# The first scores of each window with whole queries as weights and masked keys moving

## The reference

```
q, k, v = x @ wq.T + bq, x @ wk.T + bk, x @ wv.T + bv
scores  = 0 everywhere
scores[window n, window n] = q_w . k_w * 0.25      # windows of 128 tokens, 16 per batch
scores[g, g'] += q_g . k_g' * 0.25                 # 64 global tokens: every 32nd
out = softmax(scores) @ v @ wo.T + bo
x1  = layernorm(x + out)
```

## Time and profile before

| | us |
|---|---|
| median of three runs | 445.81 |
| lowest, highest | 444.01, 446.04 |
| span of the profiled execution | 442.8 |
| TensorE busy | 405.3 (92%) |
| VectorE busy | 326.1 (74%) |
| ScalarE busy | 250.6 (57%) |
| GpSimd busy | 220.4 (50%) |

### The profile page before, as it was taken

How to read it: one execution, slowest core, us unless ns; L and a number is a source line. 1 busy time by engine, 2 the same in 40 slices (tenths; PEclk the granted TensorE clock), 3 DMA queues, 4 the chain that set the end, 5 groups by cost and what they waited for, 6 DMA issues and landing times.

```text
span 442.8 us, 14658 instructions
## 1 busy us (share of the span) xinstructions
PE 405.3 (92%) x5747; PEld 339.8 (77%) x5747; DVE 326.1 (74%) x796; ACT 250.6 (57%) x523; POOL 220.4 (50%) x301
## 2 busy tenths in 40 slices
PE   5899799999999999999999899988798998999991
PEld 4758678888888888888888778756577887777891
DVE  6785687758757757757759888563668998899785
ACT  3424665675575575575576576676663555544421
POOL 4361343464464464464464566435733485477540
PEclk9999999999999999999999999999989999999997
DMA  8663740000000000000020000000000011011004
GB/s 240 186 199 111 240 137 4 27 25 0 24 24 0 24 24 0 24 24 0 24 72 4 25 2 3 3 1 2 0 2 2 1 49 47 0 47 49 34 15 143
DMA packets 21720, 20.34 MB, mean 46 GB/s; under 512 B 3133, under 2 KB 21682, under 8 KB 21682
## 3 DMA queue, kind: packets, MB, share of 16 engines
q1 hardware_dynamic: 16900, 15.07, 10.9%
q10 hardware_dynamic: 4782, 4.75, 3.3%
HBM read 15.41 MB, written 4.41 MB: 45 GB/s over the span
## 4 chain that ended last, share of the span: by engine, by line
PE 52%; DVE 26%; ACT 9%; issue 8%; DMA 3%; ACTq 1%; DVEq 0%; POOL 0%; POOLq 0%
DVE row_max_t L1154 10%; PE ps L1461 7%; PE ps L1737 7%; PE ps L1424 7%; PE ps L1562 5%; PE ps L1384 5%; PE ps L1415 4%; PE ps L1438 3%; PE ps L1444 3%; ACT probs L847 3%; DVE k_part L1013 2%; ACT boundsT_t L858 2%; PE ps L1406 2%; DMA rows<-in_L_attn_x_dram 2%; ACT k_part L713 2%
## 5 line engine op out<-in xcount | busy, mean ns | idle before, releaser
L847 ACT ACTIVATE probs<-ps 128x1024 f32<-128x1024 f32 x64 | 62.1, 1022 | 68.2 <-PE ps L1428 68.2
L1154 DVE TENSOR_REDUCE row_max_t<-ps 128x16 f32<-128x2048 f32 x31 | 70.9, 2287 | 3.7 <-PE ps L1415 3.6
L1737 PE MATMUL ps<-w_part,hm_part 128*128 128x256 f32 x384 | 53.8, 289 | 1.8 <-DVE hm_part L1332 1.8
L1415 PE MATMUL ps<-k_part,q_part 32*128 32x128 f32 x1584 | 51.5, 274 | 3.1 <-issue 1.5
L1415 PEld LDWEIGHTS ps<-k_part,q_part 32*128 32x128 f32 x1584 | 46.9, 186 | 9.2 <-issue 7.0
L1562 PE MATMUL ps<-xh_parts,w_part 128*128 128x512 f32 x192 | 53.8, 416 | 0.0
L557 POOL TENSOR_TENSOR q_part<-qf,q_part 128x512 fp32r<-128x512 f32 x32 | 41.0, 1281 | 25.7 <-ACT q_part L695 25.7
L599 POOL TENSOR_TENSOR attn_t<-num_t,rden_t 128x256 f32<-128x256 f32 x32 | 20.0, 624 | 64.7 <-DVE rden_t L1185 64.7
L1737 PEld LDWEIGHTS ps<-w_part,hm_part 128*128 128x128 f32 x384 | 48.2, 190 | 4.8 <-DVE hm_part L1332 2.4
L788 ACT ACTIVATE ffn_rows<-ps,b1s 128x512 f32<-128x512 f32 x32 | 22.0, 687 | 42.2 <-PE ps L1562 34.1
L1562 PEld LDWEIGHTS ps<-xh_parts,w_part 128*128 128x128 f32 x192 | 34.7, 194 | 6.5 <-issue 0.6
(11 more groups left out here) (234 smaller groups left out, 906.4 us busy)
## 6 DMA issues: line engine op xcount, KB each, us to landing
table<-rest_sums SPq DMA_DIRECT2D x4, 1088.0 KB, 6.1
xs<-in_L_attn_x_dram SPq DMA_DIRECT2D x16, 256.0 KB, 2.8
rows<-in_L_attn_x_dram ACTq DMA_DIRECT2D x4, 1024.0 KB, 8.1
out_dram<-yout SPq DMA_DIRECT2D x6, 512.0 KB, 2.9
w<-in_L_ffn_W_dram SPq DMA_DIRECT2D x2, 256.0 KB, 7.6
w<-in_L_ffn_W_dram SPq DMA_DIRECT2D x1, 512.0 KB, 4.2
out_dram<-yout SPq DMA_DIRECT2D x2, 256.0 KB, 2.6
out_dram<-yout ACTq DMA_DIRECT2D x2, 256.0 KB, 2.8
```

Of the source, the lines that this page charges most:

```text
L847: act.activation(probs[:, 2 * h:2 * h + 2, :], ps[:, 2 * h:2 * h + 2, :], ACT.Exp).then_inc(probs_ready, 1)
L1154: dve.tensor_reduce(row_max[:], ps_all, op=ALU.max, axis=AX.X).then_inc(max_ready, 1)
L1415: last = mm(ps[:, u, (2 * c + a) * P:(2 * c + a + 1) * P], q_part[x][quad(u), s, c, a, :], k_part[y][quad(u), s, c, :], start=(i == 0), st ...
L1737: mm(y, hm_part[a][:, 1 - p, f, c * P:(c + 1) * P], w2_part[b][:, f, :], start=(f == 0 and i == 0), stop=False)
```

## The change

The first scores take whole queries as weights and masked keys as the moving operand. The even and the odd head's keys lie side by side, 256 columns, so that one product gives two heads: 24 products in place of 48. The turned scores stay as they were, and so need masked queries too.

- ScalarE takes the query high part from PSUM with its bias (q_whole[0], two operations), now in even steps, after the exponential's argument and before the exponentials; its copy of qf in odd steps goes. VectorE takes the query remainder (q_whole[1], two operations) in place of the four of L1004, and waits for ScalarE's.
- VectorE masks the keys of the next pair (mask_keys: four tensor_scalar operations, high and low part, even and odd head) in odd steps after the guard.
- GpSimd masks the queries of the current pair (mask_queries: two tensor_scalar operations for the high part before the bounds, two for the low part after them) in even steps; q_low goes.
- The masked keys lie in the experts' xh_parts buffer, so the casts of the first group (take_high) move from step 30 to step 31; w_raw and dg change places.
- W1 lies in ysum and is loaded by SP at step 24, ahead of w2; its splitting moves to steps 26 to 28.

```diff
+        k_masked = [xh_parts[:, 0, i].rearrange("p c n -> p (c n)").rearrange("p (w c a n) -> p w c a n", w=2, c=KC, a=2)
+                    for i in range(2)]
-        qf = sb("qf", [P, 2, KC, 2, P])
+        q_whole = [sb(f"q_whole{i}", [P, SLOTS, KC, P], fp32r) for i in range(2)]
+                    for c in range(KC):                                   # SP, step 24
+                        sp.dma_start(w1[:, c, :, :], w1_dram[:, c * P:(c + 1) * P, :].rearrange("e p h -> p e h")).then_inc(ld_w1, 16)
-            def q_low(w, s):
-                need(pool, turned_scores_in_psum, w - 3)
-                pool.wait_ge(q_high_ready, w // 2 + 1)
-                pool.tensor_tensor(q_part[1][:, s], qf[:, s % 2], q_part[0][:, s].bitcast(fp32), ALU.subtract).then_inc(q_ready, 1)
+            def await_queries(w):
+                need(pool, turned_scores_in_psum, w - 2)
+                pool.wait_ge(q_ready, w // 2 + 1)
+            def mask_queries(i, s):
+                for a in range(2):
+                    pool.tensor_scalar(q_part[i][:, s:s + 2, :, a, :], q_whole[i][:, s:s + 2].bitcast(fp32), q_scale[:, a, 0:1], None,
+                                       ALU.mult).then_inc(q_masked_ready, 1)
...
             def queries_of(w, s):                                         # ScalarE
-                need(act, turned_scores_in_psum, w - 2)
-                act.wait_ge(qf_ready, w // 2 + 1)
-                copy(q_part[0][:, s:s + 2], qf[:]).then_inc(q_high_ready, 1)
+                need(act, turned_scores_in_psum, w - 3)
+                act.wait_ge(q_in_psum, w // 2 + 1)
+                for c in range(KC):
+                    last = act.activation(q_whole[0][:, s:s + 2, c, :], ps_xq[:, c * 2 * P:(c + 1) * 2 * P].rearrange("p (w n) -> p w n", w=2),
+                                          ACT.Identity, bias=bq_col[:, c:c + 1])
+                last.then_inc(q_high_ready, 1)
...
+            def queries_of(w, s):                                         # VectorE
+                dve.wait_ge(q_high_ready, w // 2 + 1)
+                for c in range(KC):
+                    last = dve.scalar_tensor_tensor(q_whole[1][:, s:s + 2, c, :], ps_xq[:, c * 2 * P:(c + 1) * 2 * P].rearrange("p (w n) -> p w n", w=2),
+                                                    bq_col[:, c:c + 1], q_whole[0][:, s:s + 2, c, :].bitcast(fp32), ALU.add, ALU.subtract)
+                last.then_inc(q_ready, 1)
+            def mask_keys(w, s):
+                need(dve, scores_in_psum, w)
+                dve.wait_ge(k_ready, w // 2 + 1)
+                for i in range(2):
+                    for a in range(2):
+                        dve.tensor_scalar(k_masked[i][:, :, :, a, :], k_part[i][:, s:s + 2].bitcast(fp32), q_scale[:, a, 0:1], None,
+                                          ALU.mult).then_inc(k_masked_ready, 1)
...
                 if ahead and p == 0:                                      # VectorE's step
-                    queries_of(t + AHEAD)
+                    queries_of(t + AHEAD, (s + AHEAD) % SLOTS)
+                if live(t + 1, steady) and p:
+                    mask_keys(t + 1, (s + 1) % SLOTS)
...
             def scores(s):                                                # TensorE
                 for c in range(KC):
+                    for i, (x, y) in enumerate(SPLIT):
+                        for u in range(UNITS):
+                            last = mm(ps[:, u, 2 * c * P:(2 * c + 2) * P], q_whole[x][quad(u), s, c, :],
+                                      k_masked[y][quad(u), s % 2, c, :, :].rearrange("p a n -> p (a n)"),
+                                      start=(i == 0), stop=(i == 2), tile_position=(32 * u, 0))
```

More of the change, by code:

```diff
@@ L503, in _ @@
             load_w(WO, wo_dram)
-            for c in range(KC):
-                sp.dma_start(w1[:, c, :, :], w1_dram[:, c * P:(c + 1) * P, :].rearrange("e p h -> p e h")).then_inc(ld_w1, 16)
             sp.dma_start(out_bias[:], bo_dram.rearrange("(a n) -> a n", a=1).broadcast_to([P, HID])).then_inc(ld_bo, 16)
@@ L574, in step @@
                 ahead, cur, pp, old, older = (live(t + k, steady) for k in (AHEAD, 0, -2, -3, -4))
+                queries_due = cur and p == 0 and (steady or t > 0)
+                if queries_due:
+                    await_queries(t)
                 if pp:
@@ L842, in step @@
                     keep_onehot(0, 0)
+                if ahead and p == 0:
+                    queries_of(t + AHEAD, (s + AHEAD) % SLOTS)
                 if prev:
@@ L1411, in scores, with scores_of_globals @@
                 for c in range(KC):
+                    for i, (x, y) in enumerate(SPLIT):
[3 more added lines that the diff above has]
+                                      start=(i == 0), stop=(i == 2), tile_position=(32 * u, 0))
+                return last
+            def scores_of_globals():
+                s = GSLOT
+                for c in range(KC):
                     for a in range(2):
@@ L1703, in _ @@
             pe.wait_ge(kg_ready, 1)
-            scores(GSLOT).then_inc(gs_in_psum, 1)
+            scores_of_globals().then_inc(gs_in_psum, 1)
             turn_x(2)
```

60 lines of the change are left out of this document (29 added, 31 removed).

## The result

464.24 us (median of 4 runs, 464.06 to 466.36) against 444.91 for the kernel before (443.33 to 446.04) on the same chip: ratio 1.045, 95% interval 1.041 to 1.049. The forecast was 446.5, range 441.5 to 453. The profiled execution has a span of 462.5 us against 442.8.

The account below looks back on a forecast made before the run. VectorE's row maximum bounds odd steps; VectorE and TensorE nearly tie in even ones. Span 442.8 +4.0 -0.2 -2.7 +0.0 -0.5 +0.5 -0.4 = 443.5; the median lies 3.0 above the span: 446.5 us, range 441.5 to 453.

Parts of the forecast that it names:

- Odd marks: First product of the turned scores in odd steps; claimed to be released by VectorE's key remainders and row maximum, not TensorE.
- the forecast's 2.7: Gain over five loop turns of two pairs each, taken from a range of 1.5 to 3.6 us.
- a lock: VectorE's masks wait for whole GpSimd operations on a shared port; loop push 0.2 becomes 0.6, start's scaling to 26.2.
- The scores: TensorE's 24 products for 48 save 0.75 us a step; odd steps gain nothing, even marks 0.16, or 0.55 at loop turns.
- VectorE's key masks: Four in odd steps at 0.43 each, 1.72 us; 1.4 hidden in idle time, 0.3 pushing the numerator and attn.
- the masks come dear: Rival: VectorE's key masks at 0.69 each, or with GpSimd between all of them, giving 455 us; chance 0.13.
- GpSimd's query masks: Four one-input operations per pair in even steps at 0.85 us each, bounds 0.66 and 1.28; cost 0.
- The rival with 1.28: GpSimd's query masks take 1.28 us; the start's lock costs 1.7 more, each loop a little: 449 us; chance 0.15.
- the odd step's spare of 0.75 us: Odd-step scores would end 0.75 us earlier than the keys need, swallowing an attn that comes 0.8 late.
- The start: Globals' scaling 2.85 to 5 us late through VectorE's queries and masks; 0.5 slack, +2.3 to +4.6, taken as +4.0.
- The end: Row maximum's wait for scores -0.5; experts' casts ahead of the routing +0.5, while leaving the row maximum's way gains 0.2.
- W1's load, VectorE's filler: W1's DMAs leaving the start's queue -0.2; in steps 24 to 28, filler moved by one step and W1's split -0.2.

Follow-up runs that it names:

- the first experiment: The changed kernel with the second pair of GpSimd's query masks moved behind attn, its bias and the centred rows: 455.26 us, ratio 1.025.
- the three moves: The changed kernel with attn ahead of the second query masks, ScalarE's step-0 queries behind the globals' exponentials, the experts' casts behind the routing: 446.5 us, 1.006.
- the last move: Second query masks directly behind attn from step 24, added to the three moves with ScalarE's first key masks and step 2's second query masks in step 1: 438.16 us.
- the best version: The three moves, ScalarE making the first key masks, step 2's second query masks made in step 1, and the last move: 438.16 us, 0.987.

## Why the prediction was wrong, step by step

**What bounds the kernel: right in the main.** Odd marks hang on VectorE's row maximum, and with attn out of the masks' way every odd mark of the loop waits for it. "In odd steps it buys nothing" is not quite so: scores and key remainders were tied to 0.1 us, and shorter scores bought 0.08 or 0.19 us at each odd mark, 1.52 in all. The 2.70 us at the even marks equal the forecast's 2.7, but by luck: it was the middle of 1.5 to 3.6, added up from 0.16 and 0.55 a mark and a lock, where 0.26 and 0.28 were measured.

**The scores: right in kind, the saving a quarter too high.** 24 products took 0.98 us, not 0.75. From their start to the start of the weighing it was 1.49 us before and is 0.91 now: 0.58 saved, where the forecast had 0.75. In even steps this made no difference, since VectorE is the limit there; odd to even is 7.77.

**VectorE's key masks: right in the loop.** They took 0.42 each against 0.43, and the rival "the masks come dear" is out there. At the start, beside GpSimd's masks, they took 0.61 each. The lock, by which each would have waited for a whole operation of GpSimd (scaling at 26.2), was not borne out with one-input masks (24.52); beside masks with two inputs such waits came.

**GpSimd's query masks: the step that failed.** It took 0.85 us, nearer the affine select than the subtraction, and bounded it by 0.66 and 1.28. The masks measured 1.57, outside the bounds; neither row was an arithmetic operation of one input (the select's ran on 8 partitions of bf16), and the kernel before has no such row on GpSimd. The rival with 1.28 gave 449, because I let the odd step's spare of 0.75 us swallow a late attn; what the first experiment leaves the scores is 0.63. No run has masks of 1.28 us ahead of attn, so that rival's price stays untested. At 1.57 the spare doesn't swallow it: two masks are 3.1 us before attn, in the loop 0.3 to 0.4 at each odd mark (3.55 over ten, of the 3.65 by which a gain of 4.22 fell to 0.57), and in steps 2, 26, 28 and 30, where VectorE's or the table's delay comes on top, 1.2 to 2.4 us each. This one order is worth 9.0 us by the first experiment.

**The start: the place right, its price half.** The forecast was +4.0 for the globals' turning, measured +4.9: 3.2 for the scaling (the prediction's own terms add up to 24.06, not 24.2), and 1.75 because TensorE took 8.51 us from the scores to the turning and not 6.76, at its granted 0.62 behind the idle time, which the sum had no term for. VectorE's shift was over at 33.26, 2.3 us before the turning: TensorE's queue ended last here, not VectorE. What it left out wholly is ScalarE's new order in step 0: its queries stood before the globals' exponentials, which made TensorE wait 2.8 us, and the keys' products behind that wait took 1.2 us more than before. Moving the queries took 3.5 us off the median, with overlapping intervals. I had costed ScalarE's part as hidden from one step of the loop, and not looked at step 0, where the exponentials of the globals share that place.

**Step 3: not seen.** Between the marks 1 and 4 I had 0. In step 2 GpSimd waits for a transfer that lands at different times, and everything put behind that wait is late by as much. With the transfer equally early, step 3 still took 3.1 us more in the changed kernel than with the three moves, so this part is the order. With the second pair's masks ahead of the wait, step 3 was 0.5 shorter than before.

**The end: one term right, one too small, one missing.** The row maximum of step 30 had -0.5, and mark 30 came after 7.47 us instead of 7.93. Mark 31 came after 11.07 instead of 8.79, by the order before attn. The casts had +0.5; they took 1.57 ahead of the routing, and what followed met GpSimd: step 32 took 9.12 us (6.37 before), and 2.9 of it was gone in the profile when they were moved (2.3 in the median, intervals overlapping).

**W1's load, VectorE's filler:** no experiment took them by themselves. In every kernel with attn ahead of the second masks and one-input masks, step 25 takes 8.7 us (8.91 before; 9.7 where the masks stand ahead of attn), so that neither costs anything there; steps 27 to 29 grew by 1.7 with VectorE's filler beside masks, and 1.3 of it came back with the last move.

So the change itself isn't slow. The loop can gain 4.2 us by it; between the changed kernel and the best version, with the same operations in another order and four key masks on ScalarE, lie 26 us.

## What to carry to other kernels

When an operation moves to another engine, take its price from a row of the same form on that engine (arithmetic or copy, how many inputs), and where none exists, let the range reach well above the dearest neighbour (here 1.57 against 1.28). Then ask of each new operation what stands behind it in the queue, in every special step and not only in the loop, and put it behind what others wait for and ahead of the engine's own long waits. A shorter operation isn't the better one if the neighbouring engine's operations get longer beside it.

## What the runs showed of the hardware

GpSimd on 128x512 fp32 from SBUF, rounded on the way out: a copy 0.61 us, a product of two inputs 1.28, by a constant 1.49, by a column's scalar 1.57. Its two-input form held VectorE's small operations for its whole length (0.16 us became 1.31); its one-input form did not (the same operation took 0.16 beside it, a cast 0.57 instead of 0.16). The Trainium skill ("SBUF — State Buffer", section "Who interferes with whom") says that a VectorE instruction with two inputs in SBUF contends with a GpSimd instruction that reads SBUF. The 1.31 us row agrees. The 0.16 us row does not: that operation also has two inputs in SBUF, and ran in the midst of a one-input mask that reads SBUF. So in these runs the form of the GpSimd instruction decides. The Trainium skill ("GPSIMD Engine Reference", section 3.1) has 769 ns for 512 elements at best, which the prediction named beside its price. No multiplication here came near it (1.28 to 1.57), and the copy was faster (0.61).

ScalarE made a key mask in 0.64 us (four in 2.56), VectorE in 0.42, GpSimd a query mask of the same size in 1.57.

TensorE's granted clock fell behind idle time of some 3 us: to 0.50 for 6 us at the start (0.62 over 8.5), and also where the idle time was moved (0.62 in 33.5 to 38). Not each time alike: with ScalarE's order changed, the scores behind the same idle time took 1.06 us and not 1.65, and the clock over the same stretch was 0.80. A wait of 2.3 us before the turning in step 30 made the weighing behind it 1.94 us instead of 1.08. So a wait on TensorE can cost more than its length: behind the wait of 2.81 us in step 0, the keys' products took 1.24 us more than before.
